# Cross-attention with a softmax over the batch: scores kept in SBUF between two passes, and the sum over the batch divided between TensorE and GpSimd

## The chip, the cores and the metric

The kernel runs on one core of one Trainium2 chip. The metric is the device time of one execution in microseconds (us). Three runs of the kernel before took 863.21, 858.28 and 855.77 us; their median, 858.28 us, is the time to compare with.

## What is computed

There are two layers. The first is a cross-attention between channels, with a softmax that runs over the batch axis and not over a row; the second is a mixture-of-experts feed-forward with two experts for each token. Cut to what matters:

```
x, ctx: (64, 128, 256) float32            # batch b, channel c, column
q      = layernorm(x)
score  = einsum('bci,bcj->bij', ctx, q) / 16      # (64, 256, 256)
score  = softmax(score, axis=0)                   # over the 64 batches
x      = x + einsum('bci,bij->bcj', ctx, score)
logits = layernorm(x) @ router_w.T ; top 2 of 8 experts, softmax of the two
x      = x + sum over both experts of prob * (gelu(xn @ w1[e].T + b1[e]) @ w2[e].T + b2[e])
```

Since the softmax runs over the batch, the maximum of every one of the 256x256 positions over all 64 batches must be known before the first exponential is taken, and the sum over all 64 exponentials before the first probability is used.

## The kernel before

A score matrix of one batch is 256x256, held as 128 partitions x 512 values. Batches are worked in pairs, so a step handles 128x1024 values and there are 32 steps (`PAIRS`) in each stage. The large SBUF tensor `slots` has one row of 514 words for each batch; `slot2(b, first, n)` are n words of each of two batches. PSUM has eight banks of 512 words. Every engine has its own program, written by hand as a `pipeline(...)` of steps in which a part with lag L works on pair m-L; engines meet in semaphores. A semaphore `m_...` belongs to the first stage, `e_...` to the second, `a_...` to the third.

**Stage 1, the maximum.** For each pair: SyncE loads x and ctx (L390, L394). VectorE takes layernorm statistics (L723, L737), GpSimd makes the reciprocal root (L457 to L462), ScalarE writes the normalised q into `slots` (L991, two activations of 128x256). TensorE makes the scores (L561, four float32 matmuls of 256 columns for a pair, which show in the trace as eight records) in a ring of two PSUM bank pairs, and VectorE folds them into `smax` (L729, L732, lag 3). The scores are then dropped. TensorE waits for `m_max` before it overwrites a bank pair.

**Stage 2, the exponentials.** For each pair SyncE loads ctx again (L402), TensorE makes the same scores again (L561), VectorE subtracts the maximum while it moves the scores from PSUM to `slots` (L756, 128x1024), and ScalarE takes the exponential in place (L998). The sum over the batch is made on two engines, two steps behind: VectorE adds 128 of the 512 columns of each batch (L752, `SUM_DVE`), GpSimd the other 384 (L482), both in SBUF in the tensor `sums`. In this stage the expert weights are also brought in: every second step TensorE transposes eight blocks (L590, L592), ScalarE writes their float16 high part (L1004, L1005), VectorE the low part (L764, L765).

At the end VectorE adds the two halves of `sums` (L770) and takes the reciprocals, columns 0 to 319 first (L773), then the rest (L774).

**Stage 3, attend.** GpSimd multiplies 320 columns of each batch by the reciprocal (L490), VectorE the other 192 (L832); TensorE transposes ctx (L607) and multiplies (L633); then come residual, layernorm and router, and rows are stored in DRAM. GpSimd's first product waits for the first reciprocal (`e_recip`).

**Stage 4, experts.** Lists of tokens are made, then 78 groups of 256 tokens go through the experts (L680, L703).

Of the kernel before, what the change touches and what calls it, by code (L numbers as in the profile page):

```python
# [51 lines left out]
SUM_DVE = 128  # L52
# [80 lines left out]
def xattn_ffn(nc, x, ctx, router_w, w1, b1, w2, b2, out):  # L133
# [7 lines left out]
    with ExitStack() as stack:  # L141
# [3 lines left out]
        def sem(name):  # L145
            return stack.enter_context(nc.semaphore(name))
# [79 lines left out]
        m_score = sem("m_score")  # L226
        m_max = sem("m_max")
# [5 lines left out]
        e_diff = sem("e_diff")  # L233
        e_exp = sem("e_exp")
        e_sumv = sem("e_sumv")
# [137 lines left out]
        L_MAX = 3  # L373
        L_SUM, L_LOW = 2, 2
# [7 lines left out]
        def _(sp):  # L382
# [26 lines left out]
            pipeline(sp, PAIRS, RING, RING, 0, load_exps)  # L409

            def attend(i, k, n):
                if live(i, k, 0, PAIRS):
                    m, r = i + k, k % RING
                    if isinstance(i, int) and i + k < RING:

                        sp.wait_ge(m_score, 2 * PAIRS)
                        sp.wait_ge(e_wT, PAIRS // 2)
# [24 lines left out]
        def _(pool):  # L442
# [30 lines left out]

            def add_up(i, k, n):
                m = i + k
                pool.wait_ge(e_exp, m + 1)
                if isinstance(m, int) and m == 0:
                    pool.wait_ge(m_top, 1)
                    pool.tensor_copy(sums[:, :, SUM_DVE:], slot2(0, SUM_DVE, 2 * DIM - SUM_DVE)).then_inc(e_sump, 1)
                else:  # L480
                    pool.wait_ge(e_sump, m)
                    pool.tensor_tensor(sums[:, :, SUM_DVE:], slot2(m * 2, SUM_DVE, 2 * DIM - SUM_DVE), sums[:, :, SUM_DVE:], ALU.add).then_inc(e_sump, 1)  # L482
            pipeline(pool, PAIRS, RING, RING, 0, add_up)
# [64 lines left out]
        def _(pe):  # L548
# [16 lines left out]
            def scores_max(i, k, n):  # L565
                m, r = i + k, k % RING
                pe.wait_ge(m_ctx_in[r], landed_at(i, k, RING))
                after(pe, m_max, m - 1)
                for j in range(2):
                    pe.wait_ge(m_q, m * 2 + j + 1)  # L570
                    score(m * 2 + j, 2 * (k % 2) + j, 2 * r + j, j == 1)
            pipeline(pe, PAIRS, RING, RING, 0, scores_max)

            def scores_exp(i, k, n):
                m, r = i + k, k % RING
                pe.wait_ge(m_ctx_in[r], landed_at(i, k, RING) + 16 * (PAIRS // RING))
# [136 lines left out]
        def _(dve):  # L713
# [4 lines left out]
            def maximum(i, k, n):  # L718
# [369 lines left out]
```

## Time and profile before

| what | value |
|---|---|
| median of the runs | 858.28 us |
| span of the profiled execution | 909.8 us |
| the profiled execution's own time | no other than its span is recorded |
| PE busy | 770.1 us (85%) |
| DVE busy | 622.8 us (68%) |
| POOL busy | 574.0 us (63%) |
| ACT busy | 390.1 us (43%) |
| stage 1 (to the end of its last maximum) | 0 to 76.6 us |
| stage 2 (to GpSimd's first product) | 76.6 to 155.3 us |
| stage 3 and the building of lists | 155.3 to about 372 us |
| stage 4 | about 372 to 909.8 us |

The profiled execution is 51.5 us longer than the median of the runs without a profile, so lengths in it stand for lengths in a run only roughly; a difference between two stretches of it is compared with its own span. PE is TensorE, PEld its weight loads, DVE VectorE, ACT ScalarE, POOL GpSimd. PEclk is the clock that TensorE was granted, as a share of 2.4 GHz. Busy time counts pieces that overlap once.

### The profile page before, as it was taken

To read this page: it belongs to the slowest core of one execution; us is meant where nothing else is said; L and a number is where in the kernel's file an instruction comes from. 1 tells how busy PE (TensorE), PEld (TensorE's weight loads), DVE (VectorE), ACT (ScalarE), POOL (GpSimd) and SP (SyncE) were. 2 spreads that over 40 slices of the span, in tenths; PEclk is the share of its full clock that TensorE was granted. 3 is DMA by queue.
4 is the path that set the end of the run, shared out by engine and by line. 5 is a ranking of instruction groups with operands and counts; after the bars stand their busy time and mean duration, and the time that the engine had idled before them with its cause. 6 is when DMAs were issued, how large, how long until landed. Compare 5 with 4: busy or idle time off the path is not lost. (4 is left out here: it accounts for less than half of the span.)

```text
span 909.8 us, 22499 instructions
## 1 busy us (share of the span) xinstructions
PE 770.1 (85%) x5931; PEld 649.5 (71%) x5932; DVE 622.8 (68%) x1520; ACT 390.1 (43%) x715; POOL 574.0 (63%) x815
## 2 busy tenths in 40 slices
PE   6999996999996449888989887989588889879886
PEld 5678885878885338766877776978367778767775
DVE  6998999899998758655655654363465656556554
ACT  3555664576666204333333433143133333334331
POOL 5664776788884056666576566366766666665663
PEclk9999997999997559999999999799789999999998
DMA  7887773488885124444344443343533343333330
GB/s 227 251 250 240 237 228 114 137 269 266 267 275 192 53 60 134 131 147 157 118 148 156 142 133 119 112 140 76 159 106 111 106 129 108 97 115 116 96 107 2
DMA packets 82200, 137.20 MB, mean 151 GB/s; under 512 B 10075, under 2 KB 55140, under 8 KB 82032
## 3 DMA queue, kind: packets, MB, share of 16 engines
q0 software_dynamic: 23104, 68.43, 24.9%
q1 hardware_dynamic: 59056, 68.26, 23.9%
q8 instruction: 22, 0.36, 0.2%
q14 instruction: 18, 0.15, 0.1%
HBM read 94.56 MB, written 47.59 MB: 156 GB/s over the span
## 5 line engine op out<-in xcount | busy, mean ns | idle before, releaser
L680 PE MATMUL psum<-work,w1T_high 128*128 128x256 f16 x1248 | 227.4, 285 | 53.5 <-ACT work L1067 36.6
L1059 ACT ACTIVATE work<-psum,slots 128x256 f32<-128x256 f32 x312 | 130.2, 471 | 309.4 <-PE psum L680 233.0
L703 PE MATMUL psum<-w2T_high,slots 128*128 x1248 | 214.7, 277 | 6.2 <-issue 5.1
L680 PEld LDWEIGHTS psum<-work,w1T_high 128*128 x1248 | 124.0, 102 | 85.9 <-issue 67.2
L680 PE MATMUL psum<-work,w1T_low 128*128 128x256 f16 x624 | 177.6, 285 | 3.5 <-issue 3.5
L703 PE MATMUL psum<-w2T_low,slots 128*128 x624 | 172.4, 276 | 1.7 <-issue 1.7
L952 DVE CAST slots<-work 128x512 f16<-128x512 f32 x156 | 71.0, 455 | 138.4 <-ACT work L1059 114.8
L703 PEld LDWEIGHTS psum<-w2T_high,slots 128*128 128x128 f16 x1248 | 119.6, 99 | 23.2 <-issue 9.2
L561 PE MATMUL psum<-slots,work 128*128 (+1 forms) x512 | 124.0, 392 | 7.4 <-ACT slots L991 6.8
L540 POOL DMA_INDIRECT rows_second<-slots x78 | 82.3, 1055 | 66.0 <-issue 35.6
L968 DVE SCALAR_TENSOR_TENSOR slots<-psum,slots 128x256 f32<-128x256 f32 x156 | 68.2, 478 | 78.5 <-remote 63.9
L540 POOL DMA_INDIRECT out_x<-slots x78 | 83.4, 1069 | 57.9 <-issue 44.9
L532 POOL DMA_INDIRECT slots<-rows_first,slots x86 | 90.0, 1047 | 45.8 <-issue 45.6
L561 PEld LDWEIGHTS psum<-slots,work 128*128 128x128 f32 x512 | 94.4, 193 | 32.1 <-issue 15.5
L954 DVE TENSOR_TENSOR slots<-work,slots 128x512 f16<-128x512 f32 x156 | 109.5, 702 | 5.4
L1067 ACT ACTIVATE work<-psum 128x1024 f16<-128x1024 f16 x78 | 80.0, 1026 | 77.3 <-remote 42.2
L532 POOL DMA_INDIRECT slots<-rows_second,slots x70 | 71.6, 1022 | 38.4 <-issue 38.4
L941 DVE SCALAR_TENSOR_TENSOR slots<-slots 128x256 f32<-128x256 f32 x156 | 69.2, 485 | 25.9 <-issue 21.3
L680 PEld LDWEIGHTS psum<-work,w1T_low 128*128 x624 | 63.8, 102 | 15.0 <-issue 5.5
L703 PEld LDWEIGHTS psum<-w2T_low,slots 128*128 128x128 f16 x624 | 61.8, 99 | 11.8 <-issue 4.1
L633 PE MATMUL psum<-slots,work 128*128 (+1 forms) x256 | 65.5, 400 | 4.3 <-DVE slots L832 4.3
L691 PE MATMUL psum<-ident,slots 128*128 128x128 f16 x624 | 50.9, 224 | 19.8 <-DMA slots<-rows_first,slots 11.5
(126 smaller groups left out, 1125.2 us busy)
## 6 DMA issues: line engine op xcount, KB each, us to landing
work<-in_ctx SPq DMA_DIRECT2D x96, 256.0 KB, 3.5
rows_first<-slots SPq DMA_DIRECT2D x32, 514.0 KB, 3.9
slots<-in_x SPq DMA_DIRECT2D x32, 256.0 KB, 3.8
work<-in_L_ffn_w SPq DMA_DIRECT2D x32, 256.0 KB, 3.2
work<-in_x SPq DMA_DIRECT2D x32, 256.0 KB, 3.1
slots<-rows_first,slots POOLq DMA_INDIRECT x86
rows_second<-slots POOLq DMA_INDIRECT x78
slots<-rows_second,slots POOLq DMA_INDIRECT x78
```

What stands on the lines that cost most here:

```text
L532: pool.indirect_dma_start(row_buf[r * SUB + s], None, source, bass.IndirectOffsetOnAxis(ap=ring_idx[:, r * 4 + s:r * 4 + s + 1], axis=0)). ...
L540: pool.indirect_dma_start(table[1] if first else out_rows, bass.IndirectOffsetOnAxis(ap=ring_idx[:, r * 4 + 2 + s:r * 4 + 3 + s], axis=0), ...
L561: mm = pe.matmul(psum[:, r2, h * DIM:(h + 1) * DIM], ctx_ring[:, place, h * P:(h + 1) * P], slot(b, 0, DIM), start=True, stop=True)
L633: mm = pe.matmul(psum[:, 2 + r, j * DIM:(j + 1) * DIM], a_ctxT[:, 2 * r + j, h * P:(h + 1) * P], slot(m * 2 + j, h * DIM, DIM), start=(h = ...
L680: mm = pe.matmul(h, w1T[pw][:, f, c, bass.ds(e * P, P)], xT[r2][:, (px * HC + c) * GROUP:(px * HC + c + 1) * GROUP], start=(c == 0 and px ...
L703: mm = pe.matmul(y, act16[r2][pa][:, f * GROUP + s * P:f * GROUP + (s + 1) * P], w2T[pw][:, f, bass.ds(e * DIM, DIM)], start=(f == 0 and p ...
L941: last = dve.scalar_tensor_tensor(rows[:, X2:X2 + DIM], b2_all[:, bass.ds(e * DIM, DIM)], rows[:, PR + now:PR + now + 1], rows[:, X2:X2 + ...
L952: dve.tensor_copy(act16[r2][0][:, cols], act32[r2][:, cols]).then_inc(x_high, 1)
L954: dve.tensor_tensor(act16[r2][1][:, cols], act32[r2][:, cols], act16[r2][0][:, cols], ALU.subtract).then_inc(x_low, 1)
L968: last = dve.scalar_tensor_tensor(rows[:, X2:X2 + DIM], psum[:, 6 + r2, s * DIM:(s + 1) * DIM], rows[:, PR + now:PR + now + 1], rows[:, X2 ...
L1059: last = act.activation(act32[r2][:, f * GROUP:(f + 1) * GROUP], psum[:, 2 + 2 * r2 + f // 2, (f % 2) * GROUP:(f % 2 + 1) * GROUP], ACT.Ge ...
L1067: act.activation(xT[r2], psum[:, 0, :].bitcast(F16), ACT.Copy).then_inc(x_xT, 1)
```

## The change

Stage 1 keeps its scores: ScalarE copies each pair from PSUM over its q in `slots`, three steps behind the queries, after VectorE has read the pair for the maximum (`m_kept`). The ring of scores in PSUM is four bank pairs (all eight banks) in place of two, and TensorE waits for `m_kept` before it overwrites one.

Stage 2 loads no ctx and makes no scores. The maximum of columns 0 to 383 is copied to a PSUM bank (`top_bank`). VectorE subtracts it in place from columns 0 to 383 of both batches (one operand in SBUF, one in PSUM), GpSimd subtracts columns 384 to 511. ScalarE's exponential waits for both. The sum is made by TensorE for columns 0 to 319 (a matmul of the identity with each batch's exponentials, 64 of them accumulated in one PSUM bank, `total`) and by GpSimd for the other 192. VectorE's first reciprocal reads `total`.

```diff
-SUM_DVE = 128
+SUM_PE = 320
+SUB_DVE = 384
+        total = psum[:, 2, 0:SUM_PE]
+        top_bank = psum[:, 1, :]
 # sync
-            def load_exps(i, k, n):
-                m, r = i + k, k % RING
-                sp.wait_ge(m_score, m + PAIRS - RING + 1)
-                sp.dma_start(ctx_ring[:, 2 * r:2 * r + 2, :], pair_of(ctx, m * 2)).then_inc(m_ctx_in[r], 16)
+            def load_weights(i, k, n):
+                m = i + k
                 if k % 2 == 0:
...
 # gpsimd
+            pool.wait_ge(m_top, 1)
+            pool.wait_ge(m_kept, PAIRS)
             def add_up(i, k, n):
-                m = i + k
-                pool.wait_ge(e_exp, m + 1)
...
-                    pool.tensor_tensor(sums[:, :, SUM_DVE:], slot2(m * 2, SUM_DVE, 2 * DIM - SUM_DVE), sums[:, :, SUM_DVE:], ALU.add).then_inc(e_sump, 1)
-            pipeline(pool, PAIRS, RING, RING, 0, add_up)
+                if live(i, k, 0, PAIRS):
+                    m = i + k
+                    pool.tensor_tensor(slot2(m * 2, SUB_DVE, 2 * DIM - SUB_DVE), slot2(m * 2, SUB_DVE, 2 * DIM - SUB_DVE),
+                                       smax[:, 0:1, SUB_DVE:].to_broadcast([P, 2, 2 * DIM - SUB_DVE]), ALU.subtract).then_inc(e_diffp, 1)
+                if live(i, k, L_SUM, PAIRS):
+                    m = i + k - L_SUM
+                    pool.wait_ge(e_exp, m + 1)
...
+                        pool.wait_ge(e_sump, m)
+                        pool.tensor_tensor(sums[:, :, SUM_PE:], slot2(m * 2, SUM_PE, 2 * DIM - SUM_PE), sums[:, :, SUM_PE:], ALU.add).then_inc(e_sump, 1)
+            pipeline(pool, PAIRS, RING, RING, L_SUM, add_up)
 # tensor
             def scores_max(i, k, n):
-                after(pe, m_max, m - 1)
+                after(pe, m_kept, m - RING + 1)
...
-                    score(m * 2 + j, 2 * (k % 2) + j, 2 * r + j, j == 1)
+                    score(m * 2 + j, 2 * r + j, 2 * r + j, j == 1)
-            def scores_exp(i, k, n):
-                m, r = i + k, k % RING
-                pe.wait_ge(m_ctx_in[r], landed_at(i, k, RING) + 16 * (PAIRS // RING))
-                after(pe, e_diff, m - 1)
-                for j in range(2):
-                    score(m * 2 + j, 2 * (k % 2) + j, 2 * r + j, j == 1)
-                if k % 2 == 0:
+            pe.wait_ge(m_max, PAIRS)
+            pe.wait_ge(m_kept, PAIRS)
+            def add_up(i, k, n):
+                if k % 2 == 0 and live(i, k, 0, PAIRS):
...
+                if live(i, k, L_SUM, PAIRS):
+                    m = i + k - L_SUM
+                    pe.wait_ge(e_exp, m + 1)
+                    for j in range(2):
+                        mm = pe.matmul(total, ident[:], slot(m * 2 + j, 0, SUM_PE), start=(isinstance(m, int) and m * 2 + j == 0),
+                                       stop=(isinstance(m, int) and m * 2 + j == BATCH - 1))
+                    mm.then_inc(e_summ, 1)
 # vector
             dve.tensor_tensor(smax[:, 0, :], smax[:, 0, :], smax[:, 1, :], ALU.max).then_inc(m_top, 1)
+            dve.wait_ge(m_kept, PAIRS)
+            dve.tensor_copy(top_bank[:, 0:SUB_DVE], smax[:, 0, 0:SUB_DVE]).then_inc(m_top, 1)
+            dve.wait_ge(m_top, 2)
             def exponentials(i, k, n):
-                if live(i, k, L_SUM, PAIRS):
-                        dve.tensor_tensor(sums[:, :, 0:SUM_DVE], slot2(m * 2, 0, SUM_DVE), sums[:, :, 0:SUM_DVE], ALU.add).then_inc(e_sumv, 1)
...
-                    dve.wait_ge(m_score, m + PAIRS + 1)
-                    dve.tensor_tensor(slot2(m * 2, 0, 2 * DIM), psum[:, 2 * r2:2 * r2 + 2, :],
-                                      smax[:, 0:1, :].to_broadcast([P, 2, 2 * DIM]), ALU.subtract).then_inc(e_diff, 1)
+                    dve.tensor_tensor(slot2(m * 2, 0, SUB_DVE), slot2(m * 2, 0, SUB_DVE),
+                                      top_bank[:, 0:SUB_DVE].unsqueeze(1).to_broadcast([P, 2, SUB_DVE]), ALU.subtract).then_inc(e_diffv, 1)
...
+            dve.wait_ge(e_summ, PAIRS)
+            dve.reciprocal(ssum[:, 0:SUM_PE], total).then_inc(e_recip, 1)
             dve.wait_ge(e_sump, PAIRS)
-            dve.tensor_tensor(ssum, ssum, sums[:, 1, :], ALU.add).then_inc(e_total, 1)
+            dve.tensor_tensor(ssum[:, SUM_PE:], ssum[:, SUM_PE:], sums[:, 1, SUM_PE:], ALU.add).then_inc(e_total, 1)
 # scalar
             def queries(i, k, n):
+                if live(i, k, L_KEEP, PAIRS):
+                    m, r = i + k - L_KEEP, (k - L_KEEP) % RING
+                    wait_apart(act, m_max, m + 1)
+                    act.activation(slot2(m * 2, 0, 2 * DIM), psum[:, 2 * r:2 * r + 2, :], ACT.Copy).then_inc(m_kept, 1)
             def exponentials(i, k, n):
-                act.wait_ge(e_diff, m + 1)
+                act.wait_ge(e_diffv, m + 1)
+                act.wait_ge(e_diffp, m + 1)
```

## Rows read from the trace of the kernel before

**Rows 1.** Busy time in stretches: us, busy (x instructions), clock, DMA share, GB/s.
```profile
core 0: us, PE busy (x) PEld busy (x) DVE busy (x) ACT busy (x) POOL busy (x), PEclk, DMA share, GB/s
...
104.00:118.00 14.00, 14.00 (x75) 11.71 (x75) 14.00 (x20) 9.59 (x13) 10.13 (x6) 1.00 0.72 230
...
152.30:157.20 4.90, 0.61 (x3) 0.21 (x2) 4.81 (x5) 0.99 (x2) 1.92 (x2) 0.50 0.50 161
157.20:164.00 6.80, 6.78 (x20) 5.60 (x21) 3.76 (x7) 0.60 (x1) 3.67 (x5) 0.56 0.16 45
164.00:333.00 169.00, 130.71 (x827) 113.23 (x825) 154.73 (x615) 96.86 (x193) 107.94 (x161) 0.85 0.62 197
```
**Rows 2.** Single lines: ns least/median/most, first and last start.
```profile
L732 DVE TENSOR_TENSOR smax<-psum,smax x31: 1204/1224/1225, 14.3 to 75.4; 128x1024 f32<-128x1024 f32 x31
L756 DVE TENSOR_TENSOR slots<-psum,smax x32: 1209/1211/1226, 77.4 to 147.7; 128x1024 f32 x28, 128x1024 f32<-128x1024 f32 x4
L752 DVE TENSOR_TENSOR smax<-slots,smax x31: 406/769/1499, 83.8 to 150.8; 128x256 f32<-128x256 f32 x31
L482 POOL TENSOR_TENSOR smax<-slots,smax x31: 1678/1683/1791, 82.1 to 150.3; 128x768 f32<-128x768 f32 x31
L490 POOL TENSOR_TENSOR slots<-slots,smax x32: 1427/1433/1747, 155.3 to 272.8; 128x640 f32 x24, 128x640 f32<-128x640 f32 x8
```
**Rows 3.** Timeline of stage 2, two steps of DVE: start, length, instruction.
```profile
142.83 0.58 ACT L1004 ACTIVATE w1T_high<-psum 128x512 f32 x1
143.18 1.21 DVE L756 TENSOR_TENSOR slots<-psum,smax 128x1024 f32 x1
143.18 1.69 POOL L482 TENSOR_TENSOR smax<-slots,smax 128x768 f32<-128x768 f32 x1 [0.26 <-POOL smax L482]
143.31 0.59 ACT L1005 ACTIVATE w2T_high<-psum 128x512 f32 x1
...
144.31 0.84 DVE L752 TENSOR_TENSOR smax<-slots,smax 128x256 f32<-128x256 f32 x1
...
146.20 0.68 DVE L764 SCALAR_TENSOR_TENSOR w1T_low<-psum,w1T_high 128x512 f32 x1
...
147.40 0.41 DVE L752 TENSOR_TENSOR smax<-slots,smax 128x256 f32<-128x256 f32 x1
...
147.73 1.21 DVE L756 TENSOR_TENSOR slots<-psum,smax 128x1024 f32 x1
```
**Rows 4.** Timeline of PE in stage 2, and its first matmuls of stage 3.
```profile
112.86 3.86 PE L561 MATMUL psum<-slots,work 128*128 x16
116.56 0.60 PE L590 MATMUL psum<-ident,work 128*128 128x128 f32 x4
...
117.43 0.87 PE L561 MATMUL psum<-slots,work 128*128 x3
...
157.22 3.75 PE L633 MATMUL psum<-slots,work 128*128 128x256 f32 x8 [4.32 <-DVE slots L832]
```
**Rows 5.** Timeline of stage 1, the way of one pair from statistics to maximum.
```profile
60.29 0.23 DVE L737 BATCH_NORM_AGGREGATE mv<-stats 128x2 f32<-128x6 f32 x2
...
62.41 1.09 ACT L991 ACTIVATE slots<-slots,shift,rstd  x2 [0.94 <-POOL shift L462]
...
64.42 1.09 ACT L991 ACTIVATE slots<-slots,shift,rstd  x2 [0.92 <-POOL shift L462]
...
65.17 1.23 DVE L732 TENSOR_TENSOR smax<-psum,smax 128x1024 f32<-128x1024 f32 x1
```
**Rows 6.** Timeline of the end of stage 2.
```profile
149.08 1.06 ACT L998 ACTIVATE slots<-slots  x1 [0.63 <-DVE slots L756]
...
150.33 1.68 POOL L482 TENSOR_TENSOR smax<-slots,smax 128x768 f32<-128x768 f32 x1 [0.94 <-ACT slots L998]
150.79 1.50 DVE L752 TENSOR_TENSOR smax<-slots,smax 128x256 f32<-128x256 f32 x1
...
153.05 2.15 DVE L773 RECIPROCAL smax<-smax 128x320 f32<-128x320 f32 x1
...
155.28 3.13 POOL L490 TENSOR_TENSOR slots<-slots,smax 128x640 f32<-128x640 f32 x2 [3.27 <-DVE smax L773]
```

More of the change, by code:

```diff
@@ L226, in xattn_ffn @@
         m_score = sem("m_score")
+        m_kept = sem("m_kept")
         m_max = sem("m_max")
@@ L232, in xattn_ffn @@
         e_wlow = sem("e_wlow")
-        e_diff = sem("e_diff")
+        e_diffv = sem("e_diffv")
+        e_diffp = sem("e_diffp")
         e_exp = sem("e_exp")
-        e_sumv = sem("e_sumv")
+        e_summ = sem("e_summ")
         e_sump = sem("e_sump")
@@ L373, in xattn_ffn @@
         L_MAX = 3
+        L_KEEP = 3
         L_SUM, L_LOW = 2, 2
@@ L414, in attend @@
                     if isinstance(i, int) and i + k < RING:
-                        sp.wait_ge(m_score, 2 * PAIRS)
+                        sp.wait_ge(m_score, PAIRS)
                         sp.wait_ge(e_wT, PAIRS // 2)
@@ L472, in _ @@
             pool.iota(quarter[:], [[TOKENS // 4, 4]], base=0, channel_multiplier=0, allow_small_or_imprecise_dtypes=True).then_inc(s_const, 1)
+            pool.wait_ge(m_top, 1)
+            pool.wait_ge(m_kept, PAIRS)
             def add_up(i, k, n):
-                m = i + k
-                pool.wait_ge(e_exp, m + 1)
[L477 to L481, printed above, removed]
-                    pool.tensor_tensor(sums[:, :, SUM_DVE:], slot2(m * 2, SUM_DVE, 2 * DIM - SUM_DVE), sums[:, :, SUM_DVE:], ALU.add).then_inc(e_sump, 1)
-            pipeline(pool, PAIRS, RING, RING, 0, add_up)
+                if live(i, k, 0, PAIRS):
[5 more added lines that the diff above has]
+                    pool.wait_ge(e_exp, m + 1)
+                    if isinstance(m, int) and m == 0:
+                        pool.tensor_copy(sums[:, :, SUM_PE:], slot2(0, SUM_PE, 2 * DIM - SUM_PE)).then_inc(e_sump, 1)
+                    else:
+                        pool.wait_ge(e_sump, m)
+                        pool.tensor_tensor(sums[:, :, SUM_PE:], slot2(m * 2, SUM_PE, 2 * DIM - SUM_PE), sums[:, :, SUM_PE:], ALU.add).then_inc(e_sump, 1)
+            pipeline(pool, PAIRS, RING, RING, L_SUM, add_up)
             pool.wait_ge(e_recip, 1)
@@ L987, in queries @@
             def queries(i, k, n):
-                m, r = i + k, k % RING
-                act.wait_ge(m_norm, m + 1)
-                for j in range(2):
-                    act.activation(slot(m * 2 + j, 0, DIM), slot(m * 2 + j, 0, DIM), ACT.Identity, bias=shift[:, r, j:j + 1],
-                                   scale=rstd[:, r, j:j + 1]).then_inc(m_q, 1)
-            pipeline(act, PAIRS, RING, RING, 0, queries)
+                if live(i, k, 0, PAIRS):
+                    m, r = i + k, k % RING
+                    act.wait_ge(m_norm, m + 1)
+                    for j in range(2):
+                        act.activation(slot(m * 2 + j, 0, DIM), slot(m * 2 + j, 0, DIM), ACT.Identity, bias=shift[:, r, j:j + 1],
+                                       scale=rstd[:, r, j:j + 1]).then_inc(m_q, 1)
+                if live(i, k, L_KEEP, PAIRS):
+                    m, r = i + k - L_KEEP, (k - L_KEEP) % RING
+                    wait_apart(act, m_max, m + 1)
+                    act.activation(slot2(m * 2, 0, 2 * DIM), psum[:, 2 * r:2 * r + 2, :], ACT.Copy).then_inc(m_kept, 1)
+            pipeline(act, PAIRS, RING, RING, L_KEEP, queries)
             def exponentials(i, k, n):
                 m = i + k
-                act.wait_ge(e_diff, m + 1)
+                act.wait_ge(e_diffv, m + 1)
+                act.wait_ge(e_diffp, m + 1)
                 act.activation(slot2(m * 2, 0, 2 * DIM), slot2(m * 2, 0, 2 * DIM), ACT.Exp, scale=SCORE_SCALE).then_inc(e_exp, 1)
```

26 lines of the change are left out of this document (8 added, 18 removed).

## The prediction

> **What bounds the kernel now.** I read the table of stretches first. In stage 2, from 104 to 118 us [rows 1], DVE is busy 14.00 of 14.00 us, PE too, ACT 9.59 and POOL 10.13; the clock is 1.00 and the DMA share 0.72, so neither transfers nor the clock set the pace. Then the single lines and the timeline, to see which of the two full engines is the cause. DVE's two steps from 143.18 to 147.73 take 4.55 us [rows 3], 2.27 us a step, and over the stage L756 starts 32 times from 77.4 to 147.7 [rows 2], also 2.27. A DVE step holds the subtraction (143.18 to 144.31: 1.13), the addition L752 and half of the two weight instructions (146.20 to 147.40: 1.20 for both, 0.60 a step). L752 needs 406 ns alone but has a median of 769 [rows 2]. The timeline shows why: the one that starts at 144.31 ends at 145.15, just behind POOL's L482 (143.18 + 1.69 = 144.87) [rows 3]. So the two additions exclude each other, while L756, with one operand in PSUM and one in SBUF, took 1209 to 1226 ns in all 32 cases [rows 2], beside a running L482 too.
> PE spaces 16 score records over 3.70 us (112.86 to 116.56), 0.231 each, and eight transposes over 0.87 (116.56 to 117.43) [rows 4]: 1.85 + 0.43 = 2.28 us a step. PE and DVE are level; relieving one alone would give nothing.
>
> Stage 1 has 31 maxima from 14.3 to 75.4 us [rows 2], 2.04 us a step. It is held by a loop of latency: statistics that end at 60.52 lead over POOL, ACT (62.41) and PE to the maximum at 65.17, which VectorE places three steps behind [rows 5]. Its maximum (1.23) and the aggregation behind it close the loop at about 6.1 us for three steps. ACT has gaps of 0.94 and 0.92 in front of its 1.09 us [rows 5].
>
> **Stage 1 after.** It adds one activation of 128x1024 a step, from PSUM, in ACT's queue. No row has it in float32. From SBUF the same size takes 1.06 (L998, [rows 6]); from PSUM half the size takes 0.59 and a queued neighbour starts after 0.48 (142.83, 143.31 [rows 3]), so twice that is 0.96 as spacing. The gap that it must fit is 0.92 to 0.94. Ends: ACT step 1.09 + 0.90 = 1.99, hidden; or no overlap and a gap of 0.1 at each wait, 1.09 + 1.06 + 0.20 = 2.35. I take 2.09, near the lower end, because ACT's queued instructions do overlap in the nearest rows: (2.09 - 2.04) x 31 = **+1.6 us**, range -1 to +9.6. Behind the copy stands the query of the next pair, and PE, then DVE wait for that; the copy's own wait, for the maximum of three steps earlier, is met long before. The four-deep ring takes no work away; it only spares PE a wait. Its wait for the kept pair is four steps old and costs nothing while ACT keeps pace.
>
> **Between the stages.** The last maximum ends at 75.4 + 1.2 = 76.6; call it M. Before, the first subtraction began 0.8 later (77.4). After, the last copy must end (M + 1.2), then the maximum is copied to PSUM (384 columns; 256 with two inputs take 0.41, I take 0.45), so DVE's first subtraction starts at M + 1.7, its exponential ends at M + 3.8, and POOL's first addition starts at M + 3.85. PE waits also, for `m_kept`.
>
> **Stage 2 after, one step of each engine.** DVE: 768 elements. From L752 alone (256: 0.41) to L756 (1024: 1.21) the slope is 1.04 ns, so 0.94, spaced 0.87; with the weights 0.60 makes 1.47. PE: four records of 320 columns at 0.231 x 320/256 = 0.29, 1.16, and 0.43 for the transposes: 1.59. ACT: 1.06 + 0.48 = 1.54 at most. POOL: L490 (640) 1.433 and L482 (768) 1.683 [rows 2] give 1.95 ns an element and 0.18 fixed, so subtraction (256) 0.68 and addition (384) 0.93: 1.61. The row of L482 shows a gap of 0.26 before it [rows 3], at a time when L752 was running, which is removed; I take 0.05 a gap, 1.72 in all. Ends: 1.61, and 0.26 twice, 2.13. **POOL sets the step, at 1.72.**
> The Trainium skill (GPSIMD Engine Reference, section 3.1) gives 4497 ns for an addition of 2048, that is 2.2 ns an element with hardly a fixed part; by that a POOL step is an estimated 1.40. That is a rival below.
> POOL's order is subtract(m), wait, add(m-2). Behind the wait stands the subtraction that the next exponential needs, but exp(m-2) is done two steps before.
>
> **The end of stage 2.** Addition 28 starts at M + 3.85 + 28T (T the step), then 0.93, subtraction 31 0.68, exponential 31 0.1 + 1.06: M + 6.65 + 28T. PE's last two matmuls with their latency take about 1.35, the reciprocal of 320 columns 2.15 [rows 6], 0.15 for two waits: POOL's first product at M + 10.3 + 28T. POOL's own last additions end by M + 9 + 28T, beside this. Before, the same product started at 155.28, M + 78.7; there the additions excluded each other once more (L752 1.50 beside L482 [rows 6]). With T = 1.72: M + 58.5. **-20.2 us.**
>
> The ctx loads (32 of 256 KB) and their issue on SP cost nothing before, with the DMA at 0.72; removing them gives nothing. The weight loads keep their buffers, and their load has more than two steps of time. Stage 3 is unchanged; its start moves.
>
> **Sum:** +1.6 - 20.2 = -18.6 us on the profiled span of 909.8, so about 891 there. The profiled span is 51.5 above the median; I take the difference unscaled, because stage 2's lengths are those of instructions: 858.3 - 18.6 = **840 us**.
>
> **Rivals.**
> 1. *ACT doesn't overlap in stage 1* (step 2.35): +9.6 in place of +1.6, 848 us. For: the gap that it must fit is no wider than the copy. Against: the queued rows. 0.13.
> 2. *Stage 2 runs at 2.1,* from POOL's gaps or from PE at its lower level (1.2 GHz) a third of the time. In rows, PE idle for over 4 us showed a clock of 0.50 and 0.56 after [rows 1], and eight records then took 3.75 [rows 4], twice their length; stage 3, with PE busy 130.71 of 169, had 0.85. The new stage has PE busy 1.59 of 1.72, with a hole of about 4 us at its start. 10.6 us back: 850. 0.12.
> 3. *POOL proportional to elements:* 1.683/768 x 640 = 1.40, PE's 1.59 sets the step: -3.6 more, 836. 0.10, inside my range.
> 4. *Slower: the new subtraction excludes POOL,* as L752 did, since its in-place operand is in SBUF. Then a POOL step is 1.61 + 0.94 + 0.26 = 2.8: M + 88.7, +10.0, and with +1.6 870 us. It decides from a step of 2.39 on. For: L752's row. Against: L756 has one SBUF operand also, and did not. 0.05. The Trainium skill (SBUF, section "Who interferes with whom") has it that a VectorE instruction contends with GpSimd's reads only with two inputs in SBUF; the trace agrees with both cases (406 against 769 ns; 1211 throughout).
> 5. *PE at 1.2 GHz throughout,* step 3.2: some 888 us. PE then is always busy, and at 104 to 118 a busy PE had 1.00. 0.02.
> 6. *No effect* (the scores were hidden anyway, something else holds at 2.27): 859. Against: both full engines lose work. 0.05.
>
> The forecast itself has 0.53. Range: 833 to 853; it holds the forecast, rivals 1 to 3 and POOL between its bounds. A measurement of this kernel tells about 1% from no change, 8.6 us. Faster by over 1% (below 849.7): 0.53 + 0.13 + 0.10 + 0.04 of rival 2 = 0.80. Within 1%: the rest of rival 2 and rival 6, 0.13. Slower: 0.07.
>
> **What would show it.** L756's successor starts 1.7 apart and not 2.27, lasts about 0.94 whether POOL runs or not; POOL is busy without gaps, DVE and PE have gaps; stage 1's maxima are 2.04 to 2.10 apart and ACT has no gap there; the first product comes at about 137 us; no row like L752 remains. It would be wrong if the first stage's step exceeds 2.2, if PE's records in stage 2 double in length, or if POOL's subtraction of 256 costs clearly more than 0.68.

## The result and the profile after

The changed kernel took 834.85 us, median of four runs (833.99 to 837.87), beside 857.81 for the kernel before (four runs, 855.77 to 863.21). The ratio is 0.9729, 95% interval 0.9691 to 0.9767: 2.7% or 23 us faster, where 18.6 us were forecast. The forecast of 840 was 5 us high, inside its range. A second comparison with the same two kernels (below, c1) gave 0.9716 (0.9684 to 0.9747).

First the single lines of the changed kernel, with columns as in [rows 2]. L747 is the maximum, L1005 the new copy, L765 and L485 the subtractions on VectorE and GpSimd, L494 GpSimd's addition, L606 TensorE's sum, L502 GpSimd's product.

```profile
L747 DVE TENSOR_TENSOR smax<-psum,smax x31: 1206/1225/1226, 14.8 to 75.8; 128x1024 f32<-128x1024 f32 x31
L1005 ACT ACTIVATE slots<-psum x32: 1000/1002/1024, 16.2 to 77.1; 128x1024 f32 x28, 128x1024 f32<-128x1024 f32 x4
L765 DVE TENSOR_TENSOR slots<-slots,psum x32: 944/948/955, 78.9 to 125.0; 128x768 f32 x28, 128x768 f32<-128x768 f32 x4
L485 POOL TENSOR_TENSOR slots<-slots,smax x32: 672/680/692, 78.3 to 125.3; 128x256 f32 x28, 128x256 f32<-128x256 f32 x4
L494 POOL TENSOR_TENSOR smax<-slots,smax x31: 917/925/944, 82.9 to 128.1; 128x384 f32<-128x384 f32 x31
L502 POOL TENSOR_TENSOR slots<-slots,smax x32: 1426/1433/1739, 131.3 to 252.4; 128x640 f32 x24, 128x640 f32<-128x640 f32 x8
```

Stage 1 is as long as it was: the maxima span 61.0 us, before 61.1 [rows 2]. The subtractions of stage 2 now take 46.1 us from first to last (78.9 to 125.0), before 70.3. Every length is the one that was worked out: 0.948 for 0.94, 0.680 for 0.68, 0.925 for 0.93. L765 lasts 944 to 955 ns in all 32 cases, so nothing shuts it out.

The stretches of stages 1 and 2, columns as in [rows 1]:

```profile
core 0: us, PE busy (x) PEld busy (x) DVE busy (x) ACT busy (x) POOL busy (x), PEclk, DMA share, GB/s
44.00:62.00 18.00, 17.48 (x73) 12.82 (x72) 17.68 (x46) 17.52 (x28) 11.84 (x37) 1.00 0.86 262
...
104.00:118.00 14.00, 14.00 (x76) 10.79 (x75) 13.84 (x19) 13.60 (x20) 14.00 (x19) 1.00 0.55 176
```

In stage 1 ACT is now busy 17.52 of 18.00 us. From 104 to 118 us four engines are at 97% or more of 14 us; before, ACT had 9.59 and POOL 10.13 [rows 1]. The clock is 1.00 in both stretches. GpSimd's own timeline there (start, length, instruction):

```profile
100.70 0.67 POOL L485 TENSOR_TENSOR slots<-slots,smax 128x256 f32 x1
101.34 0.92 POOL L494 TENSOR_TENSOR smax<-slots,smax 128x384 f32<-128x384 f32 x1
102.23 0.68 POOL L485 TENSOR_TENSOR slots<-slots,smax 128x256 f32 x1
102.88 0.92 POOL L494 TENSOR_TENSOR smax<-slots,smax 128x384 f32<-128x384 f32 x1
103.77 0.68 POOL L485 TENSOR_TENSOR slots<-slots,smax 128x256 f32 x1
```

102.23 to 103.77 is 1.54 us a step. Each instruction starts 0.03 before the one ahead of it ends: there are no gaps. This is the number that the forecast had wrong, 1.72. VectorE and TensorE in the same stretch:

```profile
100.76 1.81 DVE L765 TENSOR_TENSOR slots<-slots,psum 128x768 f32 x2
103.10 2.32 PE L606 MATMUL psum<-slots,ident 128*128 x8
103.68 1.81 DVE L765 TENSOR_TENSOR slots<-slots,psum 128x768 f32 x2
106.13 2.05 PE L606 MATMUL psum<-slots,ident 128*128 x7
```

Two steps of VectorE take 2.92 us (100.76 to 103.68), two of TensorE 3.03 (103.10 to 106.13): 1.46 and 1.51 a step, just under GpSimd's 1.54.

The kernel before was profiled a second time together with the changed one (c2, c1). With the same columns, its maximum, subtraction and GpSimd product, then TensorE's matmuls of probabilities (L633) and of the experts (L680):

```profile
L732 DVE TENSOR_TENSOR smax<-psum,smax x31: 1206/1224/1226, 13.9 to 74.9; 128x1024 f32<-128x1024 f32 x31
L756 DVE TENSOR_TENSOR slots<-psum,smax x32: 1209/1210/1226, 76.8 to 147.2; 128x1024 f32 x28, 128x1024 f32<-128x1024 f32 x4
L490 POOL TENSOR_TENSOR slots<-slots,smax x32: 1426/1432/1738, 154.7 to 276.3; 128x640 f32 x24, 128x640 f32<-128x640 f32 x8
L633 PE MATMUL psum<-slots,work x256: 377/379/774, 156.7 to 281.3; 128*128 x96, 128*128 128x256 f32 x32
L680 PE MATMUL psum<-work,w1T_high x1248: 272/273/421, 339.4 to 843.6; 128*128 128x256 f16 x179
```

The same of the changed kernel in that comparison:

```profile
L747 DVE TENSOR_TENSOR smax<-psum,smax x31: 1205/1224/1225, 13.9 to 74.9; 128x1024 f32<-128x1024 f32 x31
L502 POOL TENSOR_TENSOR slots<-slots,smax x32: 1426/1432/1739, 130.4 to 250.3; 128x640 f32 x24, 128x640 f32<-128x640 f32 x8
L648 PE MATMUL psum<-slots,work x256: 377/379/765, 133.7 to 255.0; 128*128 x96, 128*128 128x256 f32 x32
L695 PE MATMUL psum<-work,w1T_high x1248: 272/273/421, 313.6 to 819.7; 128*128 128x256 f16 x179
```

Stage 1 ends at the same time to 0.1 us. GpSimd's first product comes 24.3 us earlier (154.7, 130.4), TensorE's first matmul behind it 23.0 (156.7, 133.7), the spans are 857.9 and 833.6, 24.3 apart. In this pair of profiles the whole gain is made in stage 2 and kept to the end.

### The profile page after: what moved, and what is told of

It reads as the page before. It is cut to its first block, busy times and chain, and to the rows that moved or that the text cites. A ratio compares the mean times of both kernels' runs of the same rounds, so it can differ in the third digit from the quotient of the medians.

```text
span 832.9 us, 22173 instructions
## 1 busy us (share of the span) xinstructions
PE 731.9 (88%) x5803; PEld 621.5 (75%) x5804; DVE 599.3 (72%) x1489; ACT 413.5 (50%) x747; POOL 571.8 (69%) x847
## 4 chain that ended last, share of the span: by engine, by line
PE 31%; issue 25%; POOL 20%; DVE 12%; DMA 5%; POOLq 4%; ACT 1%; DVEq 1%; SPq 0%; ACTq 0%
PE psum L718 7%; PE psum L695 6%; POOL out_x L552 6%; POOL rows_second L552 5%; PE psum L573 5%; POOL slots L544 4%; PE psum L606 4%; POOLq L540 3%; PE psum L679 3%; DMA work<-in_ctx 2%; DVE stats L821 2%; POOL slots L538 2%; DMA slots<-rows_second,slots 1%; PE psum L648 1%; DMA slots<-rows_first,slots 1%
## 5 line engine op out<-in xcount | busy, mean ns | idle before, releaser
L695 PE MATMUL psum<-work,w1T_high 128*128 128x256 f16 x1248 | 212.2, 276 | 2.4 <-ACT work L1081 2.4
L695 PE MATMUL psum<-work,w1T_low 128*128 128x256 f16 x624 | 171.9, 276 | 0.0
L544 POOL DMA_INDIRECT slots<-rows_first,slots x86 | 93.8, 1090 | 45.8 <-issue 45.3
L552 POOL DMA_INDIRECT rows_second<-slots x78 | 80.0, 1025 | 35.2 <-issue 23.2
L552 POOL DMA_INDIRECT out_x<-slots x78 | 79.8, 1023 | 30.3 <-issue 26.2
L544 POOL DMA_INDIRECT slots<-rows_second,slots x70 | 74.0, 1058 | 38.5 <-issue 38.5
L706 PE MATMUL psum<-ident,slots 128*128 128x128 f16 x624 | 49.2, 223 | 29.1 <-DMA slots<-rows_first,slots 14.6
L573 PE MATMUL psum<-slots,work 128*128 (+1 forms) x256 | 64.8, 403 | 7.5 <-ACT slots L1000 6.9
L648 PE MATMUL psum<-slots,work 128*128 (+1 forms) x256 | 65.3, 399 | 4.7 <-DVE slots L840 4.7
L706 PEld LDWEIGHTS psum<-ident,slots 128*128 128x128 f16 x624 | 39.3, 99 | 38.4 <-DMA slots<-rows_second,slots 18.7
L695 PEld LDWEIGHTS psum<-work,w1T_low 128*128 x624 | 61.7, 99 | 7.7
```

Source lines behind the costliest of these rows:

```text
L544: pool.indirect_dma_start(row_buf[r * SUB + s], None, source, bass.IndirectOffsetOnAxis(ap=ring_idx[:, r * 4 + s:r * 4 + s + 1], axis=0)). ...
L552: pool.indirect_dma_start(table[1] if first else out_rows, bass.IndirectOffsetOnAxis(ap=ring_idx[:, r * 4 + 2 + s:r * 4 + 3 + s], axis=0), ...
L573: mm = pe.matmul(psum[:, r2, h * DIM:(h + 1) * DIM], ctx_ring[:, place, h * P:(h + 1) * P], slot(b, 0, DIM), start=True, stop=True)
L648: mm = pe.matmul(psum[:, 2 + r, j * DIM:(j + 1) * DIM], a_ctxT[:, 2 * r + j, h * P:(h + 1) * P], slot(m * 2 + j, h * DIM, DIM), start=(h = ...
L695: mm = pe.matmul(h, w1T[pw][:, f, c, bass.ds(e * P, P)], xT[r2][:, (px * HC + c) * GROUP:(px * HC + c + 1) * GROUP], start=(c == 0 and px ...
L706: mm = pe.transpose(bank[:, (c * SUB + s) * P:(c * SUB + s + 1) * P], row_buf[r * SUB + s][:, XN:XN + DIM].bitcast(F16)[:, c * P:(c + 1) * ...
```

## The experiments

Each is compared with the kernel before on the same chip; what stands beside the changed kernel is the difference of ratios, 0.001 of which is 0.86 us. The changed kernel has 0.9729 and 0.9716.

**GpSimd subtracts more, VectorE less.**

```diff
-SUB_DVE = 384
+SUB_DVE = 320
...
-                    pool.wait_ge(e_exp, m + 1)
+                    wait_apart(pool, e_exp, m + 1)
```

> The changed kernel, with GpSimd subtracting 192 of the 512 columns in place of 128, VectorE 320 in place of 384 (its wait for the exponential is written as two instructions, which costs next to nothing). Theory A (GpSimd sets the step of stage 2, at 1.535 us after the change): its subtraction goes from 0.68 (256 elements) to 0.93 (384), so the step to about 1.79 and the whole by 0.25 x 30 = +7.5 us, 842 us. Theory B (VectorE or TensorE sets the step): VectorE's subtraction falls from 0.94 to 0.81, the time stays at 835 or falls to 832.

It took 843.57 us, ratio 0.980 (0.9754 to 0.9846), some 6 us longer than the changed kernel. In the profiles GpSimd's first product comes 60.8 us after the end of the last maximum (76.1 to 136.9), in c1 54.3 (76.2 to 130.4). GpSimd's timeline in e1:

```profile
100.53 0.93 POOL L485 TENSOR_TENSOR slots<-slots,smax 128x384 f32 x1
101.42 0.93 POOL L494 TENSOR_TENSOR smax<-slots,smax 128x384 f32<-128x384 f32 x1
102.31 0.93 POOL L485 TENSOR_TENSOR slots<-slots,smax 128x384 f32 x1
```

A step is 1.78 (100.53 to 102.31), and ScalarE now waits for this line. Theory A holds: more work on GpSimd goes into the time, although VectorE had less.

**VectorE subtracts more.**

```diff
-SUB_DVE = 384
+SUB_DVE = 448
```

> The changed kernel, with VectorE subtracting 448 of 512 columns and GpSimd 64. Theory A (GpSimd sets the step now, the others are close behind): GpSimd's step falls to 0.43 + 0.93 = 1.3, VectorE's rises to 1.00 + 0.60 = 1.60, which becomes the step: 1.535 to 1.60, +2 us, 837 us. Theory B (VectorE sets it already): +0.13 x 30 = +4 us, 839 us. Theory C (GpSimd alone counts, VectorE has slack): down by 0.2 x 30 = 6 us, 829 us.

It took 838.76 us, ratio 0.9741 (0.9701 to 0.9782), 1 to 2 us above the changed kernel, which is within the interval. VectorE's timeline:

```profile
102.18 2.07 DVE L765 TENSOR_TENSOR slots<-slots,psum 128x896 f32 x2
104.17 0.68 DVE L773 SCALAR_TENSOR_TENSOR w1T_low<-psum,w1T_high 128x512 f32 x1
104.78 0.68 DVE L774 SCALAR_TENSOR_TENSOR w2T_low<-psum,w2T_high 128x512 f32 x1
105.37 1.07 DVE L765 TENSOR_TENSOR slots<-slots,psum 128x896 f32 x1
```

Two steps take 3.19 (102.18 to 105.37), 1.60 each as expected by theory A; GpSimd waits now, for ScalarE, 12 times between 84 and 122 us. Theory C, with its 829, is out; the bound has passed from one engine to the other. The median alone doesn't refute theory B, which had 839; the changed kernel's timeline does, where VectorE's step is 1.46 and so not the one that sets 1.54. The best division lies between 384 and 448 columns; e9 below tries 400.

**The maximum read from SBUF.**

```diff
-                                      top_bank[:, 0:SUB_DVE].unsqueeze(1).to_broadcast([P, 2, SUB_DVE]), ALU.subtract)
+                                      smax[:, 0:1, 0:SUB_DVE].to_broadcast([P, 2, SUB_DVE]), ALU.subtract)
```

> The changed kernel, but VectorE's subtraction reads the maximum from SBUF and not from the PSUM copy, so that both of its inputs lie in SBUF. Theory A (two SBUF inputs exclude GpSimd, as for the additions of the kernel before): VectorE's subtraction of 0.94 and GpSimd's 1.61 a step can't run side by side, the step goes from 1.535 to 2.55 or, with 0.26 at each hand-over, 2.8: +31 to +38 us, 866 to 873 us, slower than the kernel before. Theory B (VectorE's additions of before were long for another reason): same time as the changed kernel, 835 us.

It took 859.95 us, ratio 0.9979 (0.9954 to 1.0004): the whole gain is gone with one operand moved. The two subtractions:

```profile
L485 POOL TENSOR_TENSOR slots<-slots,smax x32: 673/1390/1404, 77.0 to 145.3; 128x256 f32 x28, 128x256 f32<-128x256 f32 x4
L765 DVE TENSOR_TENSOR slots<-slots,smax x32: 960/1434/1693, 77.6 to 142.8; 128x768 f32 x28, 128x768 f32<-128x768 f32 x4
```

Their medians double or grow by half, while the least lengths are about those of the undisturbed ones (672 and 944). GpSimd's subtraction of one step, and four steps later VectorE's and GpSimd's again:

```profile
98.05 1.40 POOL L485 TENSOR_TENSOR slots<-slots,smax 128x256 f32 x1
106.81 1.09 DVE L765 TENSOR_TENSOR slots<-slots,smax 128x768 f32 x1
107.04 1.40 POOL L485 TENSOR_TENSOR slots<-slots,smax 128x256 f32 x1
```

GpSimd's subtraction starts at 107.04, 0.86 before VectorE's ends (107.90), and ends at 108.44; it needs 0.68 alone, so it was held for some 0.7 us. Theory A holds in kind. In size the loss was 22 us and not 31 to 38. Once settled, four steps take 8.99 us (98.05 to 107.04), 2.25 a step and not 2.55 to 2.8; 28 x (2.25 - 1.54) is 20 of the 22. (Over the whole stage VectorE's step is 2.10, as it starts with less to wait for.) The expectation added whole lengths. Here GpSimd's subtraction ends 0.54 after VectorE's, and not 0.68, so at a change of turn some 0.14 of the next instruction has already passed, and no gap of 0.26 stands between them. The runs show this exclusion for additions and subtractions with both inputs in SBUF; no other kind of VectorE instruction was tried.

**The kernel before without VectorE's addition.**

```diff
-                    dve.wait_ge(e_exp, m + 1)
                     if isinstance(m, int) and m == 0:
+                        dve.wait_ge(e_exp, m + 1)
                         dve.tensor_copy(sums[:, :, 0:SUM_DVE], slot2(0, 0, SUM_DVE)).then_inc(e_sumv, 1)
-                    else:
-                        dve.wait_ge(e_sumv, m)
-                        dve.tensor_tensor(sums[:, :, 0:SUM_DVE], slot2(m * 2, 0, SUM_DVE), sums[:, :, 0:SUM_DVE], ALU.add).then_inc(e_sumv, 1)
...
-            dve.wait_ge(e_sumv, PAIRS)
+            dve.wait_ge(e_sumv, 1)
```

It leaves out the addition of columns 0 to 127 for all pairs but the first, so its probabilities are wrong; it serves for its time alone.

> The kernel before, with VectorE's addition in stage 2 left out for all but the first pair, so that the sum of columns 0 to 127 is not complete and 0.33 to 0.76 us a step are taken from VectorE. Theory A (TensorE is level with VectorE, at 2.28 against 2.27 a step): the step stays at 2.27 and only the last addition goes, 1.3 us or so: 856 us. Theory B (VectorE alone sets the step of 2.27): the step falls to 1.94 (GpSimd's addition) or below, -0.3 x 32 = -10 us or more, 847 us.

It took 855.82 us, ratio 0.9953 (0.9925 to 0.9981), 4 us less. In its timeline of stage 2:

```profile
104.59 0.68 DVE L762 SCALAR_TENSOR_TENSOR w2T_low<-psum,w2T_high 128x512 f32 x1
105.47 1.23 DVE L753 TENSOR_TENSOR slots<-psum,smax 128x1024 f32 x1 [0.19 <-PE psum L561]
105.71 1.69 POOL L482 TENSOR_TENSOR smax<-slots,smax 128x768 f32<-128x768 f32 x1 [0.26 <-POOL smax L482]
```

VectorE now waits for the scores, 26 times between 84 and 140 us. Its subtractions start from 77.0 to 144.4, 2.17 a step: TensorE's limit lay 0.1 under VectorE's 2.27. Theory A holds, a little less exactly than stated.

The last row also refutes one of my reasons. There is no addition on VectorE left, and GpSimd still stands for 0.26 us behind its own last addition. So the gap of [rows 3] came from GpSimd itself and not from VectorE. GpSimd runs one addition after the other in the kernel before, each behind a wait for the last one's result (`e_sump`). (The description of the kernel before puts both additions two steps behind. That holds for VectorE's alone; GpSimd's waits only for the exponential of its own pair.) Part of the 0.26 belongs to the loop. In the changed kernel the last two additions stand outside it, in the group of three that closes the stage:

```profile
125.97 3.08 POOL L494 TENSOR_TENSOR smax<-slots,smax 128x384 f32<-128x384 f32 x3
```

Three additions of 0.93 take 3.08, so each of the two gaps is some 0.15, though the second addition's exponential had ended 1.3 us before it started. In the loop of the kernel before, GpSimd's sequencer has a register instruction of 64 ns between the wait and the addition, which is part of the other 0.11; the rest of it was not traced.

**Scores kept, sum as before.** One part of the change alone; the excerpt is against the kernel before, in which `SUM_DVE` stays 128.

```diff
+SUB_DVE = 512
...
+                    act.activation(slot2(m * 2, 0, 2 * DIM), psum[:, 2 * r:2 * r + 2, :], ACT.Copy).then_inc(m_kept, 1)
...
+                    dve.tensor_tensor(slot2(m * 2, 0, SUB_DVE), slot2(m * 2, 0, SUB_DVE),
+                                      top_bank[:, 0:SUB_DVE].unsqueeze(1).to_broadcast([P, 2, SUB_DVE]), ALU.subtract).then_inc(e_diffv, 1)
...
```

> One part of the change alone: the scores are kept, stage 2 makes no scores and loads no ctx, but VectorE subtracts all 512 columns (from a full PSUM copy of the maximum) and the sum is made as before, 128 columns on VectorE and 384 on GpSimd. Theory A (VectorE is full in the kernel before, so relieving TensorE alone gives nothing): its step stays at 1.13 + 0.60 + 0.34 to 0.80 = 2.27, with +0.4 for stage 1 and +1.0 between the stages 860 us, the same as before. Theory B (TensorE was the true limit and VectorE's additions only filled its waits): the step falls to VectorE's undisturbed 2.07 or to GpSimd's 1.94, 850 us.

It took 858.23 us, ratio 0.9979 (0.9953 to 1.0006). Dropping 128 float32 matmuls and 8 MB of loads gives nothing that can be measured:

```profile
L760 DVE TENSOR_TENSOR slots<-slots,psum x32: 1206/1208/1221, 79.1 to 148.8; 128x1024 f32 x28, 128x1024 f32<-128x1024 f32 x4
L757 DVE TENSOR_TENSOR smax<-slots,smax x31: 406/782/1420, 83.9 to 151.8; 128x256 f32<-128x256 f32 x31
```

The step is 2.25 (148.8 - 79.1 over 31), and L757 is held as L752 was. Theory A holds. Together with e4: one relief alone gives 2 us (within its interval) or 4 us, both with the new division of the sum 23.

**The copy in four parts.**

```diff
-                    act.activation(slot2(m * 2, 0, 2 * DIM), psum[:, 2 * r:2 * r + 2, :], ACT.Copy).then_inc(m_kept, 1)
+                    for c in range(4):
+                        last = act.activation(slot2(m * 2, c * P, P), psum[:, 2 * r:2 * r + 2, c * P:(c + 1) * P], ACT.Copy)
+                    last.then_inc(m_kept, 1)
```

> The changed kernel, with ScalarE's copy of the kept scores in stage 1 in four activations of 256 elements in place of one of 1024: the same data, three fixed parts of some 0.1 to 0.2 us more a step. Theory A (ScalarE's step, 1.09 + 1.00 less overlap, has no room left in the 2.04 us of stage 1): +0.3 x 32 = +5 to +15 us, 842 to 850 us, with stage 1's maxima 2.2 to 2.5 apart. Theory B (ScalarE still has room, the copy is hidden): 837 us, maxima 2.04 apart.

Its four parts take 1.19 to 1.28 us from the start of the first to the end of the last, where the one took 1.00. The maxima run from 13.6 to 76.0, 2.08 a step in place of 2.03: +1.4 us in stage 1. The whole took 839.76, ratio 0.9785 (0.972 to 0.985), too wide to say more. The stretch from 20 to 60 us of the changed kernel, then of this one, columns as in [rows 1]:

```profile
20.00:60.00 40.00, 38.45 (x158) 28.19 (x157) 38.73 (x99) 38.56 (x61) 26.25 (x79) 1.00 0.85 258
20.00:60.00 40.00, 37.94 (x154) 27.41 (x153) 38.27 (x96) 39.59 (x116) 25.76 (x77) 1.00 0.78 251
```

ACT was busy 38.56 of 40 us and is now busy 39.59. That is 1.96 us of each step of 2.03, and 2.06 of each of 2.08: four parts cost 0.10 a step and not 0.25, as a queued instruction starts before the one ahead of it ends, and about half of that fitted into ScalarE's room. Neither theory holds as stated: ScalarE had little room, but four parts cost far less than the 0.3 that theory A charged, and the loss is 1.4 us and not 5 to 15.

**Aggregation before the maximum.**

```diff
                     for j in range(2):
                         dve.bn_stats(stats[:, r, j, :], slot(m * 2 + j, 0, DIM)).then_inc(m_stat, 1)
+                if live(i, k, 0, PAIRS):
+                    m, r = i + k, k % RING
+                    wait_apart(dve, m_stat, m * 2 + 2)
+                    for j in range(2):
+                        last = dve.bn_aggr(mv[:, r, j, :], stats[:, r, j, :])
+                    last.then_inc(m_mean, 1)
                 if live(i, k, L_MAX, PAIRS):
...
-                if live(i, k, 0, PAIRS):
-                    m, r = i + k, k % RING
-                    wait_apart(dve, m_stat, m * 2 + 2)
...
```

> The changed kernel, with VectorE's aggregation of a pair's statistics in stage 1 placed ahead of the maximum of three pairs earlier and not behind it. Theory A (stage 1 is held by the loop statistics - GpSimd - ScalarE - TensorE - maximum - aggregation, about 6.1 us in three steps): the loop is cut, the step falls from 2.04 to that of the next, VectorE's 1.93 plus a short wait or ScalarE's 2.00: 2.00, -1.3 us (-3 at most). Theory B (an engine is full at 2.04): no change, or +1 us for the wait between statistics and aggregation.

It took 838.24 us, ratio 0.976 (0.9703 to 0.9817). Stage 1 got longer, its maxima run from 14.3 to 78.5, 2.14 a step. The rows of the statistics and their aggregation show why:

```profile
62.65 0.25 DVE L743 BATCH_NORM_AGGREGATE mv<-stats 128x2 f32<-128x6 f32 x2 [0.22 <-DVE stats L738]
...
63.92 0.74 DVE L738 BATCH_NORM_STATS2 stats<-slots 128x6 f32 x2
64.77 0.25 DVE L743 BATCH_NORM_AGGREGATE mv<-stats 128x2 f32<-128x6 f32 x2
```

The aggregation starts 0.22 us after the statistics end, or 0.11 as in the second pair of rows (63.92 + 0.74 = 64.66), which is the commoner; without the wait it would start 0.08 before their end, as VectorE's queued instructions do. So a step is 1.93 (VectorE's own, as from 59.14 to 61.08 in the kernel before) and 0.19 to 0.31: between 2.12 and 2.24, and VectorE, without another gap, became the bound. This is theory B's wait, larger than expected. Whether the loop of latency holds stage 1 at 2.03 otherwise, the run doesn't tell; it stays argued.

**GpSimd's second product waits.**

```diff
                     m = i + k
+                    if isinstance(m, int) and m == 1:
+                        pool.wait_ge(a_probv, 1)
                     pool.tensor_tensor(slot2(m * 2, 0, PROD_POOL), slot2(m * 2, 0, PROD_POOL),
...
```

> The changed kernel, with one wait added at the start of stage 3: GpSimd's second product waits for VectorE's first. After the change VectorE's first product was shut out by GpSimd's second (it ended 1.53 us later than it could have), and TensorE's first product with it. Theory A (that lost turn delays stage 3): the first matmul of stage 3 comes 3.33 - 1.4 = 1.9 us behind GpSimd's first product, as before the change, and the whole falls by 1.4 us or a part of it. Theory B (the transfers or VectorE hold stage 3 in any case): the first matmul comes earlier, the last one doesn't.

It took 833.58 us, ratio 0.9703 (0.9633 to 0.9772). VectorE's first two products, in the changed kernel and in this one:

```profile
132.86 3.37 DVE L840 TENSOR_TENSOR slots<-slots,smax 128x384 f32<-128x384 f32 x2
132.40 1.03 DVE L842 TENSOR_TENSOR slots<-slots,smax 128x384 f32<-128x384 f32 x2
```

They take 1.03 us where GpSimd stands back, and 3.37 beside its products. TensorE's first matmul follows GpSimd's first product by 2.2 us in place of 3.3 (130.84, 133.06). Whether the whole is shorter by that can't be told at this interval.

**Both kernels again, and three small edits together.** c1 is the changed kernel and c2 the kernel before, without an edit; e9 is the changed kernel with

```diff
-SUB_DVE = 384
+SUB_DVE = 400
...
-            pool.wait_ge(m_kept, PAIRS)
+            pool.wait_ge(m_kept, PAIRS - RING + 1)
...
+                    if isinstance(m, int) and m == 3:
+                        pool.wait_ge(m_kept, PAIRS)
...
+                    if isinstance(m, int) and m == 1:
+                        pool.wait_ge(a_probv, 1)
...
-            dve.wait_ge(m_kept, PAIRS)
+            dve.wait_ge(m_kept, PAIRS - RING + 1)
...
+                    if isinstance(m, int) and m == 3:
+                        dve.wait_ge(m_kept, PAIRS)
```

> The changed kernel as it is, as the measure for the small steps of the others. Both theories: 835 us, ratio to the kernel before 0.973; stage 3 takes about 2 us longer from its first to its last matmul of probabilities than in the kernel before, if the lost turn at its start is real and no accident of one execution.

> The kernel before as it is, profiled once more. Theory A (the 909.8 us of the first profile, 51.5 above the median, lie in the expert stage of that one execution): stages 1 and 2 as in the first profile to within 0.5 us, a span of 855, the whole difference behind 336 us. Theory B (profiling lengthens this kernel everywhere): a span of 900 or more, stage 2 at 78.7 us as before.

> The changed kernel with three edits: GpSimd's second product of stage 3 waits for VectorE's first; VectorE subtracts 400 columns and GpSimd 112, which should make their steps 1.50 and 1.47; VectorE and GpSimd begin stage 2 without waiting for the last three pairs to be kept (only the PSUM bank that the maximum goes to must be free), and wait for them at their fourth subtraction. Theory A (GpSimd's step, its start and the lost turn are what is left): -1.4 for the turn, -0.035 x 30 = -1 for the step, -0.5 for the start: -2.9 us against the changed kernel of the same call, 832 us, ratio to before 0.970. Theory B (stage 3 is paced by transfers and takes back what is won ahead of it): within 1 us of the changed kernel.

c1: 835.00 us, ratio 0.9716. e9: 835.52 us, 0.9719 (0.9693 to 0.9744): no difference. Yet e9 reaches stage 3 earlier, by 2.0 of the 2.9 us expected:

```profile
L506 POOL TENSOR_TENSOR slots<-slots,smax x32: 1425/1432/1672, 129.5 to 251.8; 128x640 f32 x24, 128x640 f32<-128x640 f32 x8
L652 PE MATMUL psum<-slots,work x256: 377/379/774, 131.7 to 256.5; 128*128 x96, 128*128 128x256 f32 x32
```

Its first matmul of stage 3 comes at 131.7, 2.0 before c1's 133.7, its last at 256.5, 1.5 after c1's 255.0. This stretch took 124.8 us here, 121.3 in c1, 122.4 and 121.0 in the changed kernel's first profile and e8, 120.3 and 124.6 in the two of the kernel before. The two executions of the kernel before differ by 4 us, so a gain of 2 us ahead of this stretch can't be followed through single profiles, and my expectation in c1 that the changed kernel takes 2 us longer there is not borne out by c1 and c2. The other profiles lean towards it all the same. From GpSimd's first product to TensorE's last matmul of probabilities it is 122.2 to 122.4 us in the first profile of the kernel before, in e4 and in e5, 123.3 in e8, 124.5 to 125.8 in the changed kernel, c1, e1, e2, e3, e6 and e7; c2 (126.6) and e9 (127.0) stand outside. So the lost turn may cost some 2 us of stage 3; it isn't shown. What causes the scatter was not tried.

c2: 859.68 us with a span of 857.9. Stages 1 and 2 agree with the first profile to 0.6 us. The expert matmuls L680 took 504.2 us from first to last (339.4 to 843.6), in the first profile 559.3 (336.2 to 895.5). The 51.5 us between the first profile's span and the median thus lay in the expert stage of that one execution; profiling as such lengthens nothing (theory A).

## Why the prediction was right, step by step

- *DVE and PE are level, relieving one gives nothing.* Right: e5 relieves PE, -0.2% within its interval; e4 relieves DVE, -0.5%.
- *The two additions exclude each other, an operand in PSUM avoids it.* Right, and the heart of the change: e3 puts the operand back into SBUF and all of the gain is lost. Rival 4 did not come; its condition came true in e3, where it cost 22 us on top of the changed kernel, with a step of 2.25 and not the 2.8 that the rival has.
- *Stage 1, +1.6.* The copy took 1.00, not 1.06. ACT's own work is 1.96 us a step, under the 2.04 that it had to fit, and the maxima are as far apart as before: 0. Rival 1 did not come. The 2.09 was a choice near the lower of two ends. That a loop of latency holds the stage at 2.04 was neither shown nor refuted (e7).
- *Between the stages.* VectorE's first subtraction started 1.8 behind the end of the last maximum (77.04, 78.85), forecast 1.7: the copy to PSUM took 0.56, not 0.45.
- *DVE 1.47, PE 1.59, POOL 1.72.* DVE's step is 1.46. PE's sum records were 0.27 apart and not 0.29, its step 1.51. POOL's two instructions are 0.68 and 0.925 as worked out, but **the gaps of 0.05 were the mis-sized term**: they are -0.03, and the step is 1.54. 28 x (1.72 - 1.54) = 5.0 us. I had put the gap of 0.26 in [rows 3] down to VectorE's L752. It is GpSimd's own, between two additions of which the second waits for the first (e4), and the subtraction now stands in that place.
- *The end of stage 2.* Forecast M + 10.3 + 28T, which is 77.04 + 10.3 + 43.1 = 130.4; measured 131.3. Half of the 0.9 lies at ScalarE: its last exponential stood behind two weight copies and began at 126.58, 0.5 later than forecast, which has it 0.1 behind GpSimd's last subtraction (125.33 + 0.68). The 1.35 for PE's last matmuls, for which the prediction has no row, was 1.44 (127.63 to 129.07).
- *The sum.* Stage 1 gave 1.6 less loss and the step 5.0 more gain; 0.9 was lost in the tail: -18.6 - 1.6 - 5.0 + 0.9 = -24.3 at GpSimd's first product, as in c1 and c2. 1.3 of it did not reach TensorE: -23.0 at its first matmul. In the profile after, the reciprocal of the last 192 columns ends later behind GpSimd's start, so VectorE's first product falls behind GpSimd's second and waits for it; e8 lets it go first and gets 1.1 of the 1.3 back. That the medians also differ by 23 can't be put down to this: the spans of c1 and c2 are 24.3 apart.
- *Unscaled transfer from the profile.* Right, for a reason that I only had guessed: the surplus lay in one execution's expert stage.
- *Rival 3, a step of 1.59 by TensorE.* The time came near its 836, but by another way: TensorE's step is 1.51 and GpSimd's 1.54 sets the pace, and GpSimd's instructions have the fixed part that it denied (437, 618, 680, 925, 1433, 1683 ns for 128, 224, 256, 384, 640, 768 elements, e2 and e9 included: about 1.95 ns an element and 0.19 us).
- *Clock.* PE was idle before stage 2 began, and the profile after has

```profile
79.00:82.00 3.00, 3.00 (x14) 2.80 (x13) 2.63 (x4) 2.16 (x4) 2.31 (x4) 0.50 0.24 60
82.00:86.00 4.00, 4.00 (x20) 2.80 (x19) 3.99 (x6) 4.00 (x6) 3.22 (x6) 0.99 0.69 223
```

  so three microseconds ran at the lower level (1.2 GHz); from 86 us to the end of the stage the clock was 1.00, with PE always busy. Rivals 2 and 5 did not come. Rival 5's 888 doesn't follow from its own step of 3.2 either: 858.3 + 1.6 + (10.3 + 28 x 3.2 - 78.7) is 881.
- *The signs.* POOL without gaps, the subtraction of 0.94 whatever POOL does, and no gap on ACT in stage 1 came true. Gaps on DVE and PE hardly did (13.84 and 14.00 of 14 us), as POOL's step came down to theirs; the first product came at 131.3 and not 137.
- *The size.* The two large misses, 1.6 and 5.0 us, lie on one side, the 0.9 of the tail and the 1.3 behind GpSimd's product on the other. So the total is nearer than its terms by 2 us, and that much is luck.

## What to carry to other kernels

When two engines are full side by side, add up every engine's step before crediting a saving: here two savings of 2 and 4 us gave 23 together, once the rest was divided so that all four engines stood at 1.46 to 1.54 us. An operand that VectorE reads again and again beside a busy GpSimd is worth a copy to PSUM: 0.56 us spent, 22 saved. Where one instruction of an engine waits for the one before it, put an independent instruction between the two. And before you put a gap on an engine down to another engine, ask whether it waits for itself.

## What the runs showed of the hardware

- In e5, where stage 2 has only transposes on TensorE, eight every two steps, the granted clock was at its lower level (1.2 GHz) in every stretch from 80 to 150 us, the first two of which are

```profile
core 0: us, PE busy (x) PEld busy (x) DVE busy (x) ACT busy (x) POOL busy (x), PEclk, DMA share, GB/s
80.00:100.00 20.00, 8.57 (x37) 7.03 (x36) 20.00 (x26) 14.16 (x19) 13.76 (x9) 0.50 0.39 132
100.00:120.00 20.00, 8.53 (x36) 6.59 (x34) 20.00 (x27) 13.41 (x17) 14.34 (x10) 0.50 0.31 105
```

  Four transposes took 1.06 to 1.12 us there (0.60 in [rows 4]). TensorE, with 8.57 of 20 us busy, was far from the bound.
- Two additions on GpSimd, the second of which waits for the first, stand 0.15 us apart in straight code (changed kernel, 125.97) and 0.26 in a loop with a register instruction between (e4, 105.71); independent instructions overlap by 0.03.
- A VectorE and a GpSimd instruction that exclude each other take turns: each is longer by up to 0.7 us, and at a change of turn some 0.14 us of the next has already passed (e3).
- A copy of 1024 float32 a partition from PSUM to SBUF takes ScalarE 1.00 us; an exponential in SBUF of the same size 1.06. Cut into four, the copy takes 1.19 to 1.28, but costs its queue only 0.10 more (e6).
